# The self projections of the next group move in front of the second score half: a decoder layer with a linear attention on one core

## What is computed

```python
x = layernorm(x + mha(x, x, x, mask))          # self: 16 heads of width 8
x = layernorm(x + mha(x, ctx, ctx, None))      # cross
x = layernorm(x + relu(x @ w1 + b1) @ w2 + b2) # 128 -> 512 -> 128
q, k = elu(x), elu(ctx)
attn = (q @ (k.T @ ctx)) / (q @ k.sum(0) + 1e-6)
out = layernorm(x + attn)
# mha: softmax((q_in@qw+qb) (k_in@kw+kb)^T / sqrt(8)) (v_in@vw+vb) @ ow + ob
```

## Time and profile before

| | us |
|---|---|
| median of 3 runs | 307.82 |
| lowest and highest | 305.79, 308.09 |
| profiled execution, its own time | 308.05 |
| span of the profiled execution, first to last instruction | 306.2 |

### The profile page before, as it was taken

How to read it: one execution, slowest core, us unless ns; L and a number is a source line. 1 busy time by engine, 2 the same in 40 slices (tenths; PEclk the granted TensorE clock), 3 DMA queues, 4 the chain that set the end, 5 groups by cost and what they waited for, 6 DMA issues and landing times.

```text
span 306.2 us, 7952 instructions
## 1 busy us (share of the span) xinstructions
PE 257.2 (84%) x2850; PEld 158.1 (52%) x2850; DVE 189.7 (62%) x601; ACT 152.9 (50%) x370; POOL 115.9 (38%) x226
## 2 busy tenths in 40 slices
PE   8869659889999999999999999999999884876830
PEld 4324325455565557655765576557555653743620
DVE  6055264777748884887488758875896545344131
ACT  3004424565757465746584657475755563363220
POOL 5020230123225372437343734382438155333635
PEclk9997997999999999999999999999999978695685
DMA  3390212121211122112211221112110001000000
GB/s 106 101 259 0 60 32 77 35 61 34 80 49 29 35 79 62 32 34 76 61 34 35 71 65 31 36 47 62 31 36 20 14 0 35 19 10 2 17 0 17
DMA packets 28622, 14.45 MB, mean 47 GB/s; under 512 B 8024, under 2 KB 28200, under 8 KB 28584
## 3 DMA queue, kind: packets, MB, share of 16 engines
q1 hardware_dynamic: 27576, 13.55, 15.8%
q10 hardware_dynamic: 1008, 0.40, 0.5%
HBM read 5.33 MB, written 1.05 MB: 21 GB/s over the span
## 4 chain that ended last, share of the span: by engine, by line
PE 61%; DVE 17%; SPq 6%; issue 5%; DMA 4%; POOL 3%; ACT 2%; POOLq 0%; DVEq 0%; ACTq 0%
PE proj_ps L486 10%; PE av_ps L456 9%; DVE neg_max L817 6%; SPq L295 6%; PE proj_ps L520 6%; PE s_ps L422 4%; PE s_ps L404 4%; PE s_ps L428 4%; PE post_ps L476 4%; PE s_ps L396 4%; PE s_ps L438 3%; PE post_ps L472 3%; DMA cq_wide<-cq_lo 2%; DMA w_sb<-in_weights 2%; DVE att L847 2%
## 5 line engine op out<-in xcount | busy, mean ns | idle before, releaser
L655 ACT ACTIVATE probs<-s_ps 128x512 f32<-128x512 f32 (+1 forms) x128 | 71.9, 592 | 62.1 <-PE s_ps L438 62.1
L817 DVE TENSOR_REDUCE neg_max<-s_ps 128x4 f32<-128x512 f32 (+1 forms) x128 | 68.5, 577 | 41.9 <-PE s_ps L404 41.9
L1017 POOL TENSOR_SCALAR var_e<-mv 128x1 f32<-128x1 f32 x32 | 7.1, 223 | 101.1 <-DVE mv L868 101.1
L396 PE MATMUL s_ps<-bias_q,id_b 128*128 128x512 bf16 x64 | 20.1, 396 | 9.4 <-DVE neg_max L817 4.1
L486 PE MATMUL proj_ps<-x_t,w_sb 128*128 128x256 f32 x80 | 25.8, 447 | 0.6 <-issue 0.6
L438 PE MATMUL s_ps<-max_x,unit_sel 64*128 64x256 bf16 (+1 forms) x256 | 25.2, 276 | 0.0
L661 ACT COPY av_sb<-av_ps 128x256 f32<-128x256 f32 x32 | 11.7, 364 | 24.4 <-PE av_ps L456 24.4
L833 DVE TENSOR_TENSOR max_x<-s_ps,max_is_j 128x256 bf16<-128x256 bf16 x32 | 13.6, 425 | 14.4 <-PE s_ps L413 14.4
L1026 POOL TENSOR_TENSOR y_g<-y_n,row_sb 128x128 f32<-128x128 f32 x32 | 14.5, 454 | 18.3 <-DVE y_n L874 18.3
L456 PE MATMUL av_ps<-probs,v_aug_c 77*32 77x128 f32 x512 | 21.1, 287 | 0.0
L456 PE MATMUL av_ps<-probs,v_aug_s 128*32 128x128 f32 x512 | 20.6, 279 | 0.2 <-ACT probs L655 0.2
(11 more groups left out here) (110 smaller groups left out, 505.4 us busy)
## 6 DMA issues: line engine op xcount, KB each, us to landing
xt_in<-in_x_t SPq DMA_DIRECT2D x8, 128.0 KB, 2.3
sq_wide<-sq_hi SPq DMA_DIRECT2D x32, 32.0 KB, 1.9
sq_wide<-sq_lo SPq DMA_DIRECT2D x32, 32.0 KB, 1.9
x_all<-in_x SPq DMA_DIRECT2D x8, 128.0 KB, 2.3
cq_wide<-cq_hi SPq DMA_DIRECT2D x32, 32.0 KB, 1.9
cq_wide<-cq_lo SPq DMA_DIRECT2D x32, 32.0 KB, 1.9
out<-o_all SPq DMA_DIRECT2D x8, 128.0 KB, 1.9
sk_rows<-sk_hi SPq DMA_DIRECT2D x14, 64.0 KB, 1.9
```

Source lines behind the costliest of these rows:

```text
L396: nc.tensor.matmul(s1_ps[r][:, :], id_b[:], bias_q[:].unsqueeze(1).to_broadcast([P, RH, n]), start=True, stop=False, skip_group_check=True)
L655: nc.scalar.activation(probs[0:n, h, r, :, :, :].rearrange("p u j n -> p (u j n)"), s2_ps[r][0:n, :], ACT.Exp, scale=SCALE).then_inc(M["ex ...
L817: nc.vector.tensor_reduce(neg_max[:, b, r, RH * h:RH * (h + 1)], scores, AX_X, ALU.max, negate=True).then_inc(M["max_done"], 1)
```

## The change

The use sqk is made by TensorE at place 1 of step 0 in place of place 2: behind the transposes of the product with v and behind cv, in front of the second half of query_major. ScalarE's code for its high parts is taken out of the list of uses and pinned at place 2, where it stood. VectorE's, GpSimd's and SP's code is untouched. The bank of every use stays as it was.

```diff
     PROJ_USES = [
-        ("yc0", TAIL, 0, 0), ("cv", CROSS, 0, 1), ("sqk", NEXT, 0, 2),
+        ("yc0", TAIL, 0, 0), ("cv", CROSS, 0, 1), ("sqk", NEXT, 0, 1),
...
+                if (k, u) == (0, 2) and on(i, NEXT):
+                    wait_full(act, i, "sqk")
+                    split_hi(i, "sqk", i - NEXT, "sq", 0, C_SQB)
+                    split_hi(i, "sqk", i - NEXT, "sk", G * S, C_SKB).then_inc(M["hi_sqk"], 1)
+                    if i == NEXT:
+                        wait_read(act, i, "sqk")
+                        spread_k(act, "s", 0)
                 for name in uses_at(i, k, u):
...
-                    elif name == "sqk":
-                        wait_full(act, i, "sqk")
-                        split_hi(i, "sqk", i - NEXT, "sq", 0, C_SQB)
-                        split_hi(i, "sqk", i - NEXT, "sk", G * S, C_SKB).then_inc(M["hi_sqk"], 1)
...
```

More of the change, by code:

```diff
@@ L723, in light_work @@
                         scale_y(i, name)
-                    elif name == "sqk":
-                        wait_full(act, i, "sqk")
-                        split_hi(i, "sqk", i - NEXT, "sq", 0, C_SQB)
-                        split_hi(i, "sqk", i - NEXT, "sk", G * S, C_SKB).then_inc(M["hi_sqk"], 1)
-                        if i == NEXT:
-                            wait_read(act, i, "sqk")
-                            spread_k(act, "s", 0)
                     elif name == "cv":
```

## The result

The median rose from 308.05 us (six runs, 305.79 to 310.45) to 311.9 us (six runs, 309.49 to 313.38). The ratio is 1.0111, with a 95% interval of 1.0068 to 1.0155: the changed kernel is slower by 2.1 to 4.8 us, and the forecast of 2.65 us lies inside. The median itself, 311.9, lies inside the forecast's whole range (307.4 to 312.9) and 0.3 us above the forecast's own (309.4 to 311.6). The profiled execution of the changed kernel took 309.49 us, with a span of 307.7; it is the lowest of its six, so the two profiled spans lie closer together (306.2 and 307.7) than the medians.

A forecast was written before the change was run, and what follows sets the result against it. TensorE, with 61% of the chain of waits, was taken as the bound. 4 x 0.30 + 0.45 + 2 x 0.5 = 2.65 us on 308.05 gave 310.7, forecast as a 310.5 median; own range 309.4 to 311.6, whole range 307.4 to 312.9.

The forecast's parts named there:

- rival C: VectorE becomes the bound: the 0.66 us lateness of low parts, y_n and cross maxima comes through; 4.6 us, 312.4; chance 0.17.
- First step: At the projection's new place TensorE waits for ScalarE's read of yc0 from bank 0: 0.28 us, iterations 2 to 6.
- Second step: Behind line 404, TensorE's wait for VectorE's att before its transpose (line 472) goes: 0.16 us back, iterations 3 to 6.
- Third step: At the old place the projection no longer covers statistics and second exps: 0.18 us more, cross scores 0.30 late in all.
- Fourth step: High parts follow the exps, low parts come 0.66 us late; hidden by a later wait, SP's spread costed at nothing.
- Iterations 0 and 1: No wait at the bank; exps the projection used to cover stand open, 0.5 us each, bounds 0 to 0.96.
- A, no wait at the bank: The projection starts with ScalarE's read already done, so 5 x 0.28 us falls away: 309.1; chance 0.14.
- B, the filled wait for maxima: Before step 0's second score half the projection fills five waits of 0.51 us: 2.6 us hidden, 305.3; chance 0.06.
- D: The granted clock falls once per iteration because of each new stand: 8.2 us for five, 318.7; chance 0.03.
- E, nothing: A later TensorE stand in the same iteration takes the 0.30 us back: 307.8; chance 0.10.

The follow-up runs named there:

- experiment 1: Changed kernel with sqk ahead of cv in the table, so sqk uses bank 1: period 30.21 us (changed 30.65), one run of 311.31 us.
- experiments 3: Changed kernel with TensorE making sqk ahead of cv at place 1, same banks: period 31.09 us (changed 30.65), one run of 311.2 us.
- experiment 6: Changed kernel with ScalarE reading yc0 ahead of its first exp in step 0: period 30.42 us (changed 30.65), one run of 307.58 us.
- experiment 2: Changed kernel with sqk at place 1 in bank 1 and cv at sqk's old place, bank 0: period 30.12 us, one run of 308.35 us.
- experiment 7: Changed kernel with the move in iterations 2 to 6 alone, iterations 0 and 1 as before: period 30.65 us, one run of 312.33 us.
- experiment 5: Changed kernel with sqk in bank 1 and cv at sqk's old place, iterations 2 to 6 alone: 308.13 us, ratio 0.9989 to before, period 30.14 us.

## Why the prediction was right

The direction and the mechanism held, and the sum of the profiled pair, 2.84 us for 2.65, came out near. The likeliest case of the forecast was a change of less than 1%, and a slowdown of over 1% had 0.42; it is 1.1% that was measured. By the median alone rival C (312.4) is nearer to 311.9 than the forecast (310.5); it is the rows that decide between them.

The table takes the steady terms apart as the forecast had them, in us per iteration, from starts in iteration 3 of the changed kernel and of experiment 1, each against before (the period's row is the mean of iterations 3 to 5):

| term | forecast | changed | experiment 1 |
|---|---|---|---|
| stand in front of the projection | 0.28 | 0.38 | 0 |
| projection to the next start, against 0.96 at its old place | 0 | -0.02 | -0.09 |
| wait of line 472 gone | -0.16 | -0.16 | -0.16 |
| cover gone | 0.18 | 0.19 | 0.19 |
| sum, at the first cross scores | 0.30 | 0.39 | -0.06 |
| period | 0.30 | 0.36 | -0.08 |

The cover's line is the way from the second line 396 to line 833: 3.44 in both, against 108.86 - 104.49 = 4.37 before, of which 0.96 and 0.16 fall away. The sum is also what the start of the cross scores shows by itself: 8.19 and 7.74 us after the step's start, 7.80 before. The periods of iteration 3 alone differ from before by 0.38 and -0.07, so the sums close to 0.01.

**First step, the wait: its term was too small.** The forecast had the projection start 0.05 after ScalarE's read; it starts 0.15 after (104.70 to 104.85). That step failed in its estimate of a signal's way, which was taken from another pair of lines (476 to 859). The rest is a longer projection. Where it had to wait, the first of its four products is longer, 454 ns for 379; the tile's row (minimum, median and longest, in ns) of the changed kernel:

```profile
L486 PE MATMUL proj_ps<-xt_in,w_sb x4: 379/379/454, 104.8 to 105.6; 128*128 128x256 f32 x4
```

In experiment 1 the longest is 382. The next group follows the projection by 0.94 where it waited and 0.87 where it didn't: a stand of 0.38 and these 0.07 make the 0.45 that experiment 1 took away. The weight loads (PEld, which run beside the products) say where the 0.07 comes from. The projection's in the changed kernel, and in experiment 1:

```profile
104.82 0.73 PEld L486 LDWEIGHTS proj_ps<-xt_in,w_sb 128*128 128x128 f32 x4 [0.41 <-issue]
```

```profile
106.62 0.73 PEld L486 LDWEIGHTS proj_ps<-xt_in,w_sb 128*128 128x128 f32 x4
```

In experiment 1 the first load starts 0.10 ahead of its product (106.72), while TensorE still works on the group before. In the changed kernel it starts only 0.12 after the read's end (104.70), and 0.03 ahead of its product. From the first load to the start of the next group it is 0.97 in both (104.82 to 105.79, 106.62 to 107.59), and in experiments 3 and 6 too. So the wait holds back the weights as well as the product, and the forecast, which counted from product to product, had no term for that.

The Trainium skill, "Perfetto Trace Analysis", Optimizing Tensor Performance, Matmuls, lets rotating banks hide the evacuation. The two banks rotate before and after the change; what decides is whether ScalarE, busy with an exp, has read the bank by then. The measurement decides against taking the rule at its word.

**Second step, the wait of line 472: right.** Iteration 2, which had no such wait, is the check: there experiment 2 and before have the same period (30.12 and 30.13), where in iterations 3 to 5 they are 0.17 apart.

**Third step, the cover: right, 0.19 for 0.18.** Line 833 waits for nothing but the aggregate, and the second v product for its exps, as forecast (109.12, behind their end at 109.06). The forecast missed a small gain beside it: it gave the projection 0.96 at both places, though without a wait it takes 0.87 at the new one. The last group in front of the v product takes some 0.09 longer whichever it is (cv 0.53 for 0.43, experiment 2), so this isn't the projection's own. That gain, with the 0.16 of line 472, is why the move without the wait comes out a little better than before.

**Fourth step, the high parts: hidden in the steady iterations, but not at SP's spread in iteration 0.** The 0.66 came as forecast (line 880 at 109.83 for 109.86), line 844 has lost its wait, and nothing more came through. The sentence that the spread is wanted only two steps on, and so costs nothing, failed in iteration 0, where step 3 starts a fixed time behind the low parts: the alternative price that stood beside it, 0.66, is near what the profiled pair shows (0.72) and twice what the pair at the full clock does (0.30).

**Iterations 0 and 1: the sum near by luck.** 1.0 was forecast for both, 0.5 each; 0.87 measured, 0.83 in iteration 0 and 0.04 in iteration 1, and 0.71 of it is the keys' spread, which had been put at nothing. The exps do stand uncovered, 1.55 from line 438 to the second v product in experiment 1 as worked out. But in iteration 0 the projection also fills a wait for the maxima, and in the profiled pair it fell into the slow stretch of the clock (its row is 1.65 us, 1.13 before). Nor is the 0.04 a price of the move: in iteration 1 the low clock fell on line 396's pair before (1.06 us, 0.59 after). What the change costs there in an average execution stays open. The three traces with the early order of before took 48.86, 49.78 and 52.25 us for the two iterations, a spread wider than the 0.87, and experiment 7, meant to tell, met another clock.

**The rivals.** A, no wait at the bank, falls with the bracket of line 486. B, the filled wait for maxima, holds in iteration 0 alone, 0.30 at the full clock, and not in the five where it was priced. C, VectorE as the bound: line 472 of step 1 went from 112.10 to 112.46, no further than the cross scores did, and the 0.66 of the low parts didn't come through. D: the granted clock is 1.00 from 71 to 224 us after the change. E, nothing, falls with the period.

## What to carry to other kernels

Before moving a producer earlier, ask two things of its old and new place: has its buffer been read when it comes there, and what did it cover where it stood. A rotation of two buffers has an order, and moving one use can put it right behind the slow reader of its own buffer; exchanging two names in the table (experiment 1) took away the whole steady loss, though no whole time shows that edit by itself to be faster. To price such an edit, compare periods of the steady state between traces: they repeated to some hundredths of a us where whole times move by some us.

## What was not expected of the hardware

A wait cost more than the lateness of what it waits for: TensorE started 0.14 to 0.15 us after the end of ScalarE's read (experiment 6 and the changed kernel), where ScalarE's exps released the second v product in 0.06 (109.06 to 109.12) and TensorE's line 476 released VectorE in 0.04. And the first product after the wait took 454 ns in place of 379, its weight load 0.03 ahead of it and not 0.10. Together these made 0.22 us of price in experiment 6, for a read that ended within 0.01 of when TensorE could first have used its bank. Why this read's way is longer than that of the exps isn't shown.

The granted clock fell at different places in the first 50 us of different executions (0.99, 0.50 and 0.50 from 42 to 47 before, after and in experiment 7). Iterations 0 and 1 took 48.86 us in experiment 5 and 52.25 in experiment 7, with the same order there and another clock: 1.00 and 0.88 from 20 to 34, 0.85 and 0.50 from 47 to 51. That is more than the whole change is worth. Short stands of some 0.4 us in each iteration didn't lower it: 1.00 from 71 to 224 us.
